# TensorE's hand-over between two leaves begins on a 256-instruction boundary of its program

## The reference, cut to what matters

```python
x = x + 0.5 * ffn(layernorm(x))
x = x + attn(layernorm(x))
x = x + 0.5 * ffn(layernorm(x))

def step(carry, qkv):                 # of attn, over T = 1024 tokens of each of 8 batches
    A, M = carry
    q, k, v = qkv
    s_t = sum(k * q)
    u = k / (norm(k) + EPS)
    Au = A @ u
    denom = 1.0 + sum(u * Au)
    A = A - outer(Au, Au) / denom
    z = Au / denom
    M = M + outer(v, s_t * z)
    return (A, M), M @ q
```

## Time and profile before

| | us |
|---|---|
| three runs, median (lowest to highest) | 1108.61 (1108.02 to 1109.67) |
| the profiled execution, its own time | 1110.19 |
| the span that its trace covers | 1108.4 |
| TensorE busy | 948.0 |
| VectorE busy | 798.1 |
| ScalarE busy | 532.1 |

### The profile page before, as it was taken

The page is one execution under the profiler, slowest core; times in us unless marked ns, Lnnn a source line. Parts: engine busy times, 40 slices in busy tenths (PEclk is TensorE's granted clock), DMA queues, the critical chain, the costliest instruction groups (busy, mean ns, idle before and its releaser), DMA issues.

```text
span 1108.4 us, 28576 instructions
## 1 busy us (share of the span) xinstructions
PE 948.0 (86%) x11690; PEld 733.8 (66%) x11690; DVE 798.1 (72%) x2553; ACT 532.1 (48%) x1095; POOL 300.8 (27%) x254
## 2 busy tenths in 40 slices
PE   3799999999977698778899536692799999999998
PEld 1467777777763677676897425582667777777766
DVE  6878787777648898969359797786366666566663
ACT  4678787787741131312226212101175666566574
POOL 4355353535210000000000000000664654546340
PEclk9999999999987786969899776795799999999999
DMA  5353545455239443335443000057532433424231
GB/s 152 69 129 100 153 114 144 119 139 133 86 126 228 116 124 98 98 83 150 112 130 104 4 2 4 4 155 155 152 89 75 105 96 82 119 68 106 57 77 57
DMA packets 185522, 113.98 MB, mean 103 GB/s; under 512 B 85808, under 2 KB 178352, under 8 KB 184752
## 3 DMA queue, kind: packets, MB, share of 16 engines
q1 hardware_dynamic: 168496, 95.38, 34.1%
q10 hardware_dynamic: 16896, 16.78, 4.8%
HBM read 49.16 MB, written 37.75 MB: 78 GB/s over the span
## 4 chain that ended last, share of the span: by engine, by line
PE 33%; DVE 15%; issue 2%; ACT 1%; DMA 0%; POOL 0%; DVEq 0%; SPq 0%; ACTq 0%
PE ldl_work L1862 10%; PE ldl_work L1850 10%; DVE ldl_lane_matrix L1028 6%; DVE ldl_rank_one L1025 4%; PE ldl_work L1834 2%; DVE lane_rows L1010 2%; DVE ldl_lane_dinv L1013 2%; PE ldl_work L1426 2%; PE ldl_work L1817 1%; PE ldl_work L1804 1%; PE ldl_work L1818 1%; PE ldl_work L1436 1%; PE ldl_work L1825 1%; PE ldl_work L1798 1%; PE ldl_work L1186 1%
## 5 line engine op out<-in xcount | busy, mean ns | idle before, releaser
L1612 POOL TENSOR_TENSOR T<-T,out_bv_rows 128x512 f32<-128x512 f32 x16 | 20.4, 1273 | 453.1 <-DVE out_s_over_d L1715 447.1
L382 DVE TENSOR_TENSOR ffn_h_rest<-ffn_ps_h,ffn_h_high 128x512 f16<-128x512 f32 x128 | 87.0, 684 | 53.8 <-ACT ffn_ps_h L552 53.3
L551 ACT ACTIVATE ffn_h_high<-ffn_ps_h,b_columns 128x512 f16<-128x512 f32 x128 | 87.8, 686 | 64.7 <-PE ffn_ps_h L625 64.1
L1862 PE MATMUL ldl_work<-w_ternary,ldl_panels 128*128 128x256 f16 x512 | 118.2, 273 | 0.0
L639 PE MATMUL ffn_ps_y<-w_ternary,ffn_h_rest 128*128 128x256 f16 x512 | 117.8, 273 | 0.0
L639 PE MATMUL ffn_ps_y<-w_ternary,ffn_h_high 128*128 128x256 f16 x512 | 117.8, 273 | 0.0
L625 PE MATMUL ffn_ps_h<-ffn_xT_high,w_ternary 128*128 128x512 f16 x256 | 98.7, 386 | 12.0 <-DVE ffn_h_rest L382 12.0
L625 PE MATMUL ffn_ps_h<-ffn_xT_rest,w_ternary 128*128 128x512 f16 x256 | 98.3, 384 | 0.0
L1850 PE MATMUL ldl_work<-out_xT_high,w_ternary 128*128 128x512 f16 x256 | 97.1, 379 | 0.0
L1850 PE MATMUL ldl_work<-out_xT_rest,w_ternary 128*128 128x512 f16 x256 | 97.1, 379 | 0.0
L1763 ACT ACTIVATE ldl_work<-ldl_work,b_columns 128x512 f32<-128x512 f32 x128 | 84.1, 657 | 0.0
(11 more groups left out here) (211 smaller groups left out, 2325.3 us busy)
## 6 DMA issues: line engine op xcount, KB each, us to landing
ffn_x<-in_x SPq DMA_DIRECT2D x16, 512.0 KB, 4.7
x_scratch<-ffn_x_out ACTq DMA_DIRECT2D x16, 512.0 KB, 3.3
aT_scratch<-ffn_aT SPq DMA_DIRECT2D x16, 512.0 KB, 5.4
inv_aT<-aT_scratch SPq DMA_DIRECT2D x16, 512.0 KB, 4.8
ldl_panels<-uT_scratch SPq DMA_DIRECT2D x32, 256.0 KB, 3.0
T<-x_scratch SPq DMA_DIRECT2D x16, 512.0 KB, 3.8
uT_scratch<-ffn_uT SPq DMA_DIRECT2D x16, 256.0 KB, 5.4
inv_uT<-uT_scratch SPq DMA_DIRECT2D x16, 256.0 KB, 4.4
```

The costliest lines, as they stand in the source:

```text
L382: nc.vector.tensor_tensor(hl[n % 2][:, f], ps_h[f % 3][:], hh[n % 2][:, f], ALU.subtract).then_inc(hl_done, 1)
L551: nc.scalar.activation(hh[n % 2][:, f], ps_h[f % 3][:], ACT.Gelu, bias=c.b1[:, f:f + 1])
L1862: ins = nc.tensor.matmul(ps_y[t % 2], part[k % 2][:, f, t * P:(t + 1) * P], c.w2[:, f], start=(f == 0 and part is hh), stop=(f == FC - 1 a ...
```

## The change

```diff
@@ -1254,6 +1254,8 @@
             k = r - 1
             work = area(r, "diagonal")
             emptied_of(pe, k, "panel")
+
+            pe.addr_align(256, max_nops=0)
             pe.wait_ge(turned, r)
             for p, q in tile_order():
                 i = nc.tensor.matmul(work[rows_of(q), p, W:2 * W], Tt[rows_of(q), :, p],
```

## The result

The changed kernel is slower: 1122.03 us, the median of 6 runs (1115.74 to 1124.54), against 1110.31 of 6 runs of the kernel before beside it (1108.02 to 1112.42). The ratio is 1.0100, with 1.0079 to 1.012 for its 95% interval: +11.7 us where +3.8 was forecast.

What follows compares the result with a forecast made beforehand. Leaf, hand-over, leaf was taken to bound the kernel, with TensorE waiting for instruction blocks. Release -0.4, edges +0.75 and third hand-over +3.4 gave +3.75, say +3.8, on 1108.61: 1112.4 us, range 1106.5 to 1116.6.

Steps and rivals of the forecast that it cites:

- where the edges go: Hand-overs other than the third: 513 instructions from slot 0 reach a third block; 5.5 us each, +0.75 us over five.
- What bounds the kernel: Leaf, hand-over, leaf in sequence; TensorE waits at block edges, each block usable 3.83 or 4.19 us after the previous one.
- the lone last pass in slot 512: Second round's last product, raising diag_done, stands first in a third block; expected alone, some 0.3 us late in other hand-overs.
- The step that failed: Third block requested at slot 256, about +1.8 us, usable 3.5 us later; last product at +5.2 to +5.3.
- The upper bound of 6.3: Longest hand-over outside the third: 1.8 us to slot 256, 4.19 for the slowest gap without heavy traffic, 0.33 to the leaf.
- The third hand-over: Three block gaps, behind the jump, before the second round and before the last product: leaf at 485.0 for 481.66, +3.4 us.
- The rival of one more late fetch ahead of the jump: Third hand-over: the block before also arrives late, one more gap of 3.9 us precedes the jump; 1116.3 us, chance 0.12.
- The release: First load itself waits, without a separate wait instruction: 0.08 us saved in each of five hand-overs, -0.4 us.
- The filling: Slots skipped ahead of each hand-over run nowhere; the jump costs an instruction in idle time; some 97 packets for 92.
- The rival in which the jump throws the fetched block away: At the jumps: slot 0 is fetched only from the jump; +3.0 in the second hand-over, 1115.4 us; jump's cost, chance 0.09.
- the rival without effect: Whole kernel: loader's boundary is not the fetch's, or the third's loss balances the others' gain; 1108.6 us, chance 0.16.
- The rival in which the third hand-over escapes its stops: Third hand-over: an earlier request gets TensorE through L1246 in time, 5.6 us for 9.18; 1105.3 us, chance 0.11.

Runs made afterwards that it cites:

- e4: The changed kernel with its directive's alignment set to 1 slot, so nothing is filled and no edge moves: 1110.23 us, ratio 0.9991 to the kernel before.
- e10: e8 plus, in the second factorisation, a directive of alignment 1 that puts the wait for turned on the first load: 1114.87 us, ratio 1.0041 to the kernel before.
- e8: The changed kernel with the directive kept at the third hand-over alone, first load in slot 0: 1120.7 us, ratio 1.0092 to the kernel before.
- e3: The changed kernel without the directive at the third hand-over, the other five kept at slot 0: 1119.06 us, ratio 1.0073 to the kernel before.
- e9: Directive in the second factorisation only: slot 239 at its first hand-over, alignment 1 at the other two: 1112.24 us, ratio 1.0009 to the kernel before.
- e5: The changed kernel with first loads in slots 4, 8, 16, 32, 64 at hand-overs one, two, four, five, six, no directive at the third: 1118.71 us.
- e6: As e5 with the slots dealt otherwise, 64, 32, 8, 4, 16 at hand-overs one, two, four, five, six: 1116.33 us.

## Why the prediction was right or wrong, step by step

**Right: the direction, and where the edges go.** The range was missed on its upper side by 5.4 us. What bounds the kernel, the packets (97), the 0.05 us of release, the lone last pass in slot 512 and the picture of the third hand-over came as put.

**The step that failed** is this sentence: "The third block is asked for when the list reaches slot 256, which is near the end of the first round." From it came 5.5 us for a hand-over and 6.3 for its upper bound. Slot 256 is the separate wait for the second round, and the request goes out only once that wait is over: the packet is at some +4.0, the product 2.5 us later at +6.5, the leaf 0.33 behind that at 6.8, and 6.67 to 6.92 were measured. The mechanism, a third block that is late, was right; the term was given as +0.35 (+0.75 - 0.4) and measured +6.52. The upper bound of 6.3 had the same start in it, so it did not bound the unknown: the slowest gap was added to a start that no row showed. The fifth hand-over before, from which the 3.5 us were read, has its edge within the first round, and the next separate wait over 100 instructions on; that row priced another case. In the two profiles this term is 6.2 us of the 7.5 by which the forecast was short (11.3 between the spans for 3.8).

**The third hand-over** was given +3.4 and has +3.18 (12.36 - 9.18), by its three steps: the first product 4.95 us after L1039 by the gap behind the jump, the second round 0.29 late, the last pass behind a stop of 1.77. That the sizes agree is partly luck: the block with the end of L1246 came 1.46 us after L1039 where 0.26 was assumed, the gap behind it was 3.49 for 4.19, and the layout without the change gave from 8.57 to 10.30. The rival of one more late fetch ahead of the jump, another 3.9 us, did not occur.

**The release** came as put: the first load goes 0.05 us after L1039 for 0.14. By itself it is too small to be measured: e4, which has nothing else, stands at 0.9991 with 1 inside its interval.

**The filling** hid as put: the jump takes 2.25 to 3.65 us ahead of hand-overs four to six, all of it within a leaf. The Trainium skill says that a taken branch forces a fetch of its target when that lies outside the fetched window ("Runtime: NRT & Kernel Launch", Instruction fetch mechanics). Every jump here goes to the start of the next block, so no run shows one that leads further. What the trace shows is in line with it: the jump took 0.30 us ahead of the first hand-over, where the next block was there, and 3.29 to 3.65 ahead of the third, fifth and sixth, where it wasn't. The rival in which the jump throws the fetched block away fell with that, and the rival without effect fell with the ratio. The rival in which the third hand-over escapes its stops did not occur in any layout tried: it never took less than 8.57 us.

**Not foreseen: the clock.** A later third hand-over was counted as its own length, and what follows it was put at nothing without a reason. L1186 behind the last leaf took 2.72 us more at the lower level, +2.42 in the stretch. The prediction had no term for a thing that idles longer and then runs slower. TensorE idles 2.1 us longer ahead of that leaf's turn (3.84 for 1.75), since its work beside the leaf was done 38.7 us after the leaf's start for 40.8 before: L1186 there took 5.63 us for 6.30, L1206 with its stops 10.6 for 11.3, and the products for q and v waited 0.70 us for transfers instead of 1.48. The kernels' second profiles have 39.3 for 40.9.

**Open.** Why a wait close behind an edge holds the request was not shown, only that it does and that e10, without the wait, has no hold. What its reach is measured in is open too: between 8 and 32 instructions where the edge was passed at full pace, between 62 and 70 behind a stop (but 70 ahead of the sixth hand-over of e8 was held, by the wait for `turned`). Neither the number of instructions alone nor TensorE's time alone tells these apart. Why e3's fifth got through at 0 is not known. No version here was measured faster than the kernel before: e4 and e9 cannot be told from it.

## What to carry to other kernels

Where TensorE runs small products, count the edges of its 256-instruction blocks through the stretch that everything waits for, and see that no edge lies within some 30 instructions ahead of a separate wait, or some 70 if the engine stops at that edge: the wait holds the fetch of the next block, and the engine paid 1.3 to 2.0 us at the next edge. An instruction that carries its only semaphore itself does not do this, so an edge right behind such a load (slot 255 here) is the good place within a hand-over, and slot 0 the bad one when the stretch is 513 long; the total gained from neither. Alignment in one place moves all edges behind it, up to the next directive: read the whole list again, since one directive at the third hand-over cost 6.3 us in the fifth and sixth (17.60 for 11.31). And when a cost is a start plus a gap, bound the start as well as the gap.

## What the runs showed of the hardware

- A separate semaphore wait shortly behind a block's edge delays the instruction packet for the next block: in the changed kernel it moves +3.99 to +4.37 us after L1039, in e5 and e6 with 32 or 64 instructions between at +2.34 to +2.55. With the wait on the load itself the delay is gone (e10 against e8).
- The reach of such a wait is longer where the engine had stopped at the edge: 24 to 62 instructions were held there (e3, e5, e6, e8), 70 and 72 were not (e8, before).
- From the packet to the pass that needed it 2.3 to 3.0 us go by (five hand-overs each in the changed kernel's two profiles).
- A taken jump to the start of the next block took 0.30 us where that block was there, and 1.8 to 3.65 us ahead of the other five hand-overs (changed kernel).
- 128 passes of 32 x 128 took 3.72 us at a granted clock of 1.00 and 5.03 to 6.47 at a mean of 0.71 to 0.54, the first after at most 1.87 us of idle time ahead of the leaf's turn, the others after 2.34 or more.
